# Cross-attention and FFN megakernel, one core: the third input part's norm set up ahead of the trunk, and ScalarE's copy of turned probabilities put ahead of the even step's exponential

## The reference

```
x = x + L0_xattn(keys=ctx, queries=layernorm(x), values=ctx)   # 16 heads of 64, causal softmax
x = x + L0_ffn(layernorm(x))        # FP4-quantised gate/up/down, hidden 352
x = x + L1_xattn(layernorm(x), ctx) # two softmaxes: keys 0..76 and 77..127, summed, plus bias
x = x + L1_ffn(layernorm(x))        # router, top 2 of 8 experts, hidden 512
```

## Time and profile before

| what | value |
|---|---|
| median of 3 runs | 686.27 us (685.11 to 691.33) |
| profiled execution, its own time | 689.11 us |
| its span, first to last instruction | 687.1 us |
| mean granted TensorE clock | 0.983 of full |

### The profile page before, as it was taken

One profiled execution on the slowest core, in us unless ns is written; L12 is line 12 of the kernel. 1 busy time (PEld: TensorE's weight loads), 2 busy tenths in 40 slices (PEclk: granted clock), 3 DMA queues, 4 the chain that ended last, 5 costly groups with the idle time before them and its releaser, 6 DMA issues.

```text
span 687.1 us, 16668 instructions
## 1 busy us (share of the span) xinstructions
PE 623.5 (91%) x5849; PEld 569.1 (83%) x5849; DVE 530.4 (77%) x1446; ACT 438.2 (64%) x1125; POOL 305.1 (44%) x437
## 2 busy tenths in 40 slices
PE   5788989989888999999999999999999997979980
PEld 5677878878878888999999989988888977969980
DVE  5789996788888988889899897797666675655655
ACT  4777788777777776665565655555755545646760
POOL 2465434343434343353434342335327575465550
PEclk9999999999999999999999999999999999999995
DMA  9700000000000000316666041000001001212215
GB/s 228 234 2 1 2 2 2 1 2 1 1 2 1 2 18 1 124 42 127 121 112 125 2 120 36 1 2 1 2 1 32 25 24 49 63 55 60 74 51 187
DMA packets 49470, 33.28 MB, mean 48 GB/s; under 512 B 9494, under 2 KB 45948, under 8 KB 49388
## 3 DMA queue, kind: packets, MB, share of 16 engines
q1 hardware_dynamic: 47116, 27.55, 17.1%
q0 software_dynamic: 2272, 4.67, 2.0%
HBM read 17.57 MB, written 14.63 MB: 47 GB/s over the span
## 4 chain that ended last, share of the span: by engine, by line
PE 53%; DVE 15%; issue 12%; ACT 9%; POOL 7%; DMA 2%; another core or an unknown queue 1%; SPq 0%; POOLq 0%; DVEq 0%; ACTq 0%
PE ps_s L756 6%; PE ps_j L587 6%; PE ps_h L830 5%; PE ph L1684 5%; ACT scores L968 5%; PE ps_t L794 5%; PE py L1695 4%; PE ps_j L367 4%; PE ps_h L809 4%; DVE scores L1236 4%; PE ps_j L369 3%; PE ps_j L368 3%; POOL probs L1511 3%; POOL xs_scratch L1611 3%; DVE neg_max L1243 3%
## 5 line engine op out<-in xcount | busy, mean ns | idle before, releaser
L1511 POOL TENSOR_TENSOR probs<-scores,rsums 128x308 f32<-128x308 f32 (+1 forms) x192 | 153.9, 816 | 224.9 <-DVE rsums L1256 223.8
L1251 DVE TENSOR_REDUCE sums<-scores 128x4 f32<-128x308 f32 (+1 forms) x192 | 90.7, 500 | 28.7 <-ACT scores L968 23.4
L794 PE MATMUL ps_t<-ident,probs 128*128 128x128 f32 x512 | 78.4, 275 | 24.5 <-ACT probsT L984 21.8
L968 ACT ACTIVATE scores<-scores,neg_max 128x128 f32<-128x128 f32 x256 | 81.6, 394 | 21.9 <-DVE neg_max L1243 21.7
L855 ACT ACTIVATE QT<-ps_j 128x512 f32<-128x512 f32 x64 | 38.3, 598 | 80.4 <-PE ps_j L369 80.3
L794 PEld LDWEIGHTS ps_t<-ident,probs 128*128 128x128 f32 x512 | 57.7, 140 | 31.4 <-issue 26.2
L984 ACT ACTIVATE probsT<-ps_t 128x512 f32<-128x512 f32 x128 | 75.5, 590 | 5.8 <-PE ps_t L794 5.8
L756 PE MATMUL ps_s<-KT,QT 64*128 64x128 f32 x1024 | 75.7, 288 | 0.8 <-ACT KT L861 0.8
L809 PE MATMUL ps_h<-probsT,V 128*64 128x128 f32 x1024 | 70.0, 279 | 1.2 <-DVE x_sb L1016 1.1
L756 PEld LDWEIGHTS ps_s<-KT,QT 64*128 64x128 f32 x1024 | 63.3, 190 | 8.8 <-issue 2.4
L830 PE MATMUL ps_h<-Wo,headsT 128*128 128x128 f32 x512 | 69.1, 278 | 0.0
(11 more groups left out here) (240 smaller groups left out, 1615.7 us busy)
## 6 DMA issues: line engine op xcount, KB each, us to landing
xs_scratch<-xs SPq DMA_DIRECT2D x8, 1032.0 KB, 8.3
xt<-xs_scratch SPq DMA_DIRECT2D x39, 64.5 KB
w1b<-in_L_ffn_w_dram SPq DMA_DIRECT2D x1, 2048.0 KB, 8.2
big_raw<-in_L_ffn_w_dram SPq DMA_DIRECT2D x8, 256.0 KB, 5.0
ysum<-y_scratch SPq DMA_DIRECT2D x4, 512.0 KB, 5.3
Wo<-in_L_xattn_Wo_dram SPq DMA_DIRECT2D x2, 512.0 KB, 4.9
out_dram<-x_sb SPq DMA_DIRECT2D x4, 256.0 KB, 2.3
x_sb<-in_x_dram SPq DMA_DIRECT2D x3, 256.0 KB, 9.2
```

Of the source, the lines that this page charges most:

```text
L794: ins = nc.tensor.transpose(ps_pT[:, j * S:(j + 1) * S], probs[s % 2][:, j, :], ident[:, :])
L968: ins = nc.scalar.activation(scores[s % 4][:, j, :], scores[s % 4][:, j, :], ACT.Exp, bias=neg_max[:, s % 4, 0, j:j + 1])
L1251: ins = nc.vector.tensor_reduce(sums[:, p4, i, :], scores[p4][:, :, k0:k1], AX_X, ALU.add)
L1511: ins = nc.gpsimd.tensor_tensor(probs[(s - 1) % 2][:, :, k0:k1], scores[r][:, :, k0:k1], rsums[:, r, i, :].rearrange("p (h a) -> p h a", a ...
```

## The change

Three edits.

1. The third part. VectorE's statistics(2) run ahead of the trunk, right after statistics(1), instead of in step 1. GpSimd's rstd, centring and scaling of part 2 run ahead of the trunk too, behind those of part 1 (whose scaling moves from step 0), instead of in steps 2 and 3. On SP's queue the load of x part 2 goes ahead of the three loads of weight halves 3, 4 and 5. PART_AT for part 2 is 0 instead of 1, so its transposes and ScalarE's split come in step 3 instead of 4 and VectorE's low halves in step 4 instead of 5.
2. One weight part later: w0_low(5) goes from step 1 to step 2 on VectorE.
3. In even steps of both layers ScalarE makes the copy probsT (with its waits for the transposes and for the heads) right after the copy KT and ahead of the exponential, instead of after the exponential and the slots. Odd steps are as before.

```
--- before.py
+++ after.py
@@ -381,7 +381,7 @@
         def part_of(g):
             return next(p for p, (b0, nb) in enumerate(PARTS) if b0 <= g * PAIR < b0 + nb)
 
-        PART_AT = {1: -2, 2: 1, 3: 7, 4: 11}
+        PART_AT = {1: -2, 2: 0, 3: 7, 4: 11}
         QUANT_FROM, QUANT_TO = 7, 22
         WT_AT, WT_LOW = (16, 18, 22), (17, 19)
 
@@ -485,6 +485,7 @@
             for j in (1, 2):
                 w0_low(dve, j)
             statistics(dve, 1)
+            statistics(dve, 2)
 
         def over_width(v, nb):
             return v.rearrange("p (b a) -> p b a", a=1).broadcast_to([P, nb, D])
@@ -943,6 +944,13 @@
                     router_silu(u, 2)
                     router_silu(u, 3)
 
+            def copy_probs(n, s, G, first):
+                if (s >= 2 or not first) and s - 2 < STEPS:
+                    act.wait_ge(SS["pT_ready"], n - 1)
+                    wait_pos(act, SS["heads_ready"], G * BLOCKS + (s - 6) // 2 + 1)
+                    nc.scalar.activation(probsT[(s - 2) % 4][:, :, :].rearrange("p h s -> p (h s)"),
+                                         ps_pT[:, :], ACT.Copy).then_inc(SS["pT_copied"], 1)
+
             def step(G, g, s, lay, prev, first=False, last=False, nxt=None, f=None, fd=None):
                 n = G * STEPS + s
                 if s < STEPS:
@@ -956,6 +964,8 @@
                 if s < STEPS:
                     if par == 0 and (hb + 1 < BLOCKS or not last):
                         copy_k(m + 1, (hb + 1) % BLOCKS)
+                    if par == 0:
+                        copy_probs(n, s, G, first)
                     if par == 1:
                         act.wait_ge(SS["v_ready"], m + 1)
                         wait_pos(act, SS["heads_ready"], m - 1)
@@ -978,11 +988,8 @@
                 slot(**f)
                 for u, t in routes(n):
                     route_mid(u, t)
-                if (s >= 2 or not first) and s - 2 < STEPS:
-                    act.wait_ge(SS["pT_ready"], n - 1)
-                    wait_pos(act, SS["heads_ready"], G * BLOCKS + (s - 6) // 2 + 1)
-                    nc.scalar.activation(probsT[(s - 2) % 4][:, :, :].rearrange("p h s -> p (h s)"),
-                                         ps_pT[:, :], ACT.Copy).then_inc(SS["pT_copied"], 1)
+                if s % 2 == 1 or s >= STEPS:
+                    copy_probs(n, s, G, first)
                 if s % 2 == 0 and (s >= 4 or not first) and s < STEPS + 4:
                     mr = G * BLOCKS + (s - 4) // 2
                     act.wait_ge(SS["heads_ready"], mr + 1)
@@ -1277,13 +1284,13 @@
                         if i - 2 < len(now):
                             quantise_weights(now[i - 2])
                     for p, t in parts_at(n):
-                        if t == 0 and i == 3:
+                        if t == 0 and i == 3 and n > 0:
                             statistics(dve, p)
                         if t == 4 and i == 0:
                             part_low(dve, p)
                     if n == 0 and i in (2, 3):
                         w0_low(dve, i + 1)
-                    if n == 1 and i == 2:
+                    if n == 2 and i == 2:
                         w0_low(dve, 5)
                     slot(part=i, **f)
                     slot(part=i, **fd)
@@ -1536,10 +1543,10 @@
                     nc.gpsimd.tensor_tensor(lo[:, cols], big_raw[:, cols], hi[:, cols].bitcast(F32),
                                             ALU.subtract).then_inc(split, 1)
                 for p, t in parts_at(n):
-                    if t == 1:
+                    if t == 1 and p > 2:
                         rstd_part(pool, p)
                         center_part(pool, p)
-                    if t == 2:
+                    if t == 2 and p > 2:
                         scale_part(pool, p)
                 blank(n - GROUPS * STEPS)
                 if n >= ROUTE_FROM[0]:
@@ -1618,8 +1625,10 @@
                        {124: range(0, 2), 125: range(2, 4), 126: range(4, 6), 128: range(6, 8)}]
 
             stage(0, 0, 0)
-            rstd_part(pool, 1)
-            center_part(pool, 1)
+            for p in (1, 2):
+                rstd_part(pool, p)
+                center_part(pool, p)
+                scale_part(pool, p)
             return trunk(pool, step), rstd_of, twin, send
 
 
@@ -1905,9 +1914,9 @@
             load_w0(2)
             load_x(1)
             load_ctx(1)
+            load_x(2)
             for j in (3, 4, 5):
                 load_w0(j)
-            load_x(2)
             load_ctx(2)
             sp.wait_ge(s_fz, 1)
             for i, w in enumerate((w_gate, w_up)):
```

## The result

The changed kernel took 683.92 us (median of 20 runs, 681.42 to 687.96) against 687.24 us of the kernel before in the same runs: ratio 0.9952 [0.9936, 0.9967], 3.3 us faster where 6.4 was forecast. Run again on two other occasions it gave 0.9928 [0.9902, 0.9953] and 0.9933 [0.991, 0.9956], 4.9 and 4.6 us. The direction was right; about half of the size came in the first comparison, three quarters in the others.

A forecast was written before the change was run, and what follows sets the result against it. TensorE bounds layer 1; in layer 0 TensorE, ScalarE and VectorE form one loop, VectorE fuller early. Start -3.35 and layer 0 copy -3.1, layer 1 nothing, sum to -6.4 us: 680 us, range 675.5 to 687.

The forecast's parts named there:

- The start, -3.35 (or -1.8 if the clock falls): Up to step 6: less idle time in step 3 and faster step 4 bring step 6 3.35 us earlier, or 1.8.
- The chance of 0.12 for a fall: Rival at step 4: the clock falls again, the start gives only 1.8 us, time 681.4; chance 0.12.
- The links: Steps 1 to 3: sums at about 19.4 us, copy probsT at 20.9, TensorE's new wait of about 2 us.
- The copy in layer 0, +0.6 - 3.7 = -3.1: Layer 0: probsT ahead of the exponential costs 0.6 us by step 24, then gains 3.7 in eight pairs.
- the eight named pairs: Steps 30, 32, 36, 42, 46, 52, 56, 62: the copy fits ScalarE's idle time, gaining 0.46 us each on average.
- the 0.2 us lost in 34, 44 and 54: Layer 0, these three steps: TensorE loses 0.2 us each, made good in the next pair.
- the forecast pieces: Steps 6 to 22, where VectorE is full: single losses and returns at each step, leaving +0.6 us at step 24.
- The rival by which all 21.8 us come back: Whole span: all of TensorE's wait for the copy probsT is regained, time 664.5 us; chance 0.05.
- In layer 1 I cost the edit at nothing: All of layer 1: TensorE has no gap to give and the later exponentials stay covered, so edit 3 costs 0.
- step 70: Layer 1 example: its exponential moves from 294.46 to about 296.35 us, with 0.5 us of cover before VectorE's sums.
- One sign of being wrong: After step 64: a difference to the kernel before that shrinks, instead of some 6 us unchanged to the end.

The follow-up runs named there:

- c2_changed: The changed kernel again, unedited, on the same chip as e12: 682.70 us, ratio 0.9933 to the kernel before.
- e5: The changed kernel with probsT ahead of the even exponential only up to step 4 and from 24 to 110: 680.81 us, ratio 0.9903.
- e8: The changed kernel with the copy headsT also ahead of the exponential in eight late-input pairs: 679.72 us, ratio 0.9903.
- e4: The changed kernel with part 2's transposes back in step 4 and its low halves in step 5: 684.49 us, ratio 0.9923.
- e7: The changed kernel with the edits of both e5 and e4: 680.56 us, ratio 0.9903.
- e9: The changed kernel with 14 more, unneeded matmuls in step 3 ahead of the part transposes: 682.71 us, ratio 0.9941.
- e11: e7 with the copy headsT also ahead of the exponential in six pairs of layer 0: 676.57 us, ratio 0.9857.
- e3: The changed kernel with the copy probsT back behind the exponential from step 112 on: 684.79 us, ratio 0.9915.
- e12: The changed kernel with the copy probsT back behind the exponential in steps 114 and 118 only: 680.07 us, ratio 0.9894.
- c0_changed: The changed kernel again, unedited, on another occasion: 681.98 us, ratio 0.9928 to the kernel before.
- e1_start: The changed kernel with edits 1 and 2 only, the copy probsT behind the exponential everywhere: 686.93 us, ratio 0.9955.
- c1_before: The kernel before again, unedited, for a second profile: 685.72 us, one run.
- e10: The kernel before with the copy probsT ahead of the even exponential only from step 112 on: 690.50 us, ratio 1.0052.
- e2: The changed kernel with edit 3 only, edits 1 and 2 taken back: 686.42 us, ratio 0.9949.

## Why the prediction was half right

**The start, -3.35 (or -1.8 if the clock falls): both sizes right, the credit in part misplaced.** Where step 0 took 2.08 us as in the profile of before, and the clock held in step 4, c2_changed, e5 and e8 stand at -3.65, -3.61 and -3.51 (e4, e7, e9 and e11 lie near them); where it fell, the changed kernel, e3 and e12 at -1.58, -1.81 and -1.66. What was missing is a third case, a step 0 at the full pace already: -4.97 in c0_changed. In the three profiles of the changed kernel each case came once. The chance of 0.12 for a fall was too low: of the ten profiles with the new start and a slow step 0 it fell in three; in both profiles of before it fell as well. The links (sums, copy, new wait of about 2 us) were right within 0.2 us. But the prediction had edit 3 bring the copy forward in step 3; e1_start shows that TensorE's wait shrinks without edit 3 too, since the part transposes cover the copy.

**The copy in layer 0, +0.6 - 3.7 = -3.1: right, the first term in part by luck.** The distance from step 6 to 64 changed by -3.30, -3.32 and -3.34 us in the three profiles of the changed kernel: +0.33 to step 24, -3.65 behind it. Pair by pair, from the distances of c2_changed: seven of the eight named pairs gave 0.46 to 0.71 us, pair 30 gave nothing, 0.14 us each came ahead of steps 26 and 30, and the 0.2 us lost in 34, 44 and 54 came as forecast. Ahead of step 24 the forecast pieces did not all come: step 6 was to lose 0.48 and gained 0.14, step 14 lost 0.68 for 0.5, step 16 lost 0.11 for 0.65, and 18 gave nothing back for 0.49; the errors largely cancel in the sum. e5 shows that the early part is a loss of the copy's place there (0.04 without it), e8 that headsT was the next limit, as the earlier trace rows said. The rival by which all 21.8 us come back fell with it.

**"In layer 1 I cost the edit at nothing": the step that failed.** Up to step 114 it held, at -0.2. But I followed only the loop of scores, probabilities and heads, took step 70 for all of layer 1, and looked for who waits for the exponential among VectorE's sums. Behind the exponential on ScalarE stands, in steps 114 and 118, also the router's hidT, and behind that TensorE. One sign of being wrong that the prediction named came with it: the distance shrinks after step 64, from 6.98 to 3.39 us in c2_changed. The two waits are 0.48 + 0.85 = 1.33 us. In the profiles the loss from 114 to 122 is 2.4 us (changed) and 3.8 to 3.9 us (c0, c2), where c1_before moved by 0.2; what exceeds the waits goes with the low clock. Alone it costs 3.6 us [2.0, 5.2] by e10.

**The sum.** For c2_changed: -3.65 + 0.33 - 3.67 - 0.22 + 3.83 = -3.38 us at step 122. For c0_changed -4.66, for the first profile -2.73: -3.6 in the mean, beside a measured 3.3 to 4.9. With layer 1 at nothing, as forecast, c2 would stand at -7.0, close to the -6.4. In the first profile two terms missed: the start stands at -1.58 instead of -3.35, since the clock fell there, and layer 1 at +2.1 instead of nothing (-0.21 to step 114, +2.36 behind it).

**What stays open.** How the copy's place in the routed steps brings the clock down. Of the eight profiles that have the hidT waits, seven had low clock between 490 and 550 us; of the eight without them, two. The mean granted clock of all executions, on record for every run, says the same. e10's nine lie at 0.975 to 0.978, the fourteen of before on the same chip at 0.976 to 0.982, medians 0.977 and 0.980; 0.003 of 690 us is 2.1 us, and with the waits' 1.33 that is 3.4 of the measured 3.6 (an estimate from these rows). On the chip of c0, c2, e9, e5, e7 and e12, 4 of the 35 executions with the waits reached 0.982, and 16 of the 18 without. On the chip of e1 to e4, e3 and e4 show no such distance (medians 0.980 and 0.981). So the copy's place there costs clock; that the waits are the way is not shown: e3 and e12 fell without them, e2 kept the clock with them, and in the changed kernel's first profile the fall at 522 us came 8 us behind the wait. How often each case of the start comes isn't known either, and the gain by the runs hangs on it: e1's profile, with the early clock, took 684.11 us, well under the median of its own runs (686.93), so its -5.2 us isn't what that kernel gives on the whole.

## What to carry to other kernels

When a wait is put ahead of other work on an in-order engine, list everything behind it in every kind of step, not in a typical one; the costly case may stand in two steps of a hundred. Before counting a stall as gain, read what the stalled engine needs next: 1.42 us of wait held 0.5 us of gain until headsT moved too. And compare distances step by step over two or three profiles of the same kernel: here the terms that repeated to 0.05 us were the edit's, and those that didn't held the clock.

## What the runs showed of the hardware

The clock at the start differs between executions of one kernel. Step 0's sixteen score matmuls at 11.0 us took 1.16 us in c0_changed and 2.08 us in c2_changed, whose rows are otherwise alike:

```profile
11.03 2.08 PE L757 MATMUL ps_s<-KT,QT 64*128 64x128 f32 x16 [0.78 <-ACT KT L862]
...
22.99 0.63 PE L416 MATMUL pf<-ident,ctx_sb 128*128 128x128 f32 x4 [1.88 <-DVE xnT_lo L471]
...
31.11 1.16 PE L757 MATMUL ps_s<-KT,QT 64*128 64x128 f32 x16
```

That is worth 1.3 us at step 6, and behind the same idle 1.9 us the clock fell in one of the three profiles, worth 2 us more. The level at the start is read from these lengths: the profile's clock column prints 1.00 there in every kernel, also where the same 16 matmuls took 2.08 us. The Trainium skill's page "TensorE: Matmul & The Clock Gate", Part 1, says that the point of the change varies with when the first matmul lands, by some half microsecond; the trace agrees that it varies, and differs in size: in c0_changed the matmuls are at the full pace from 11.04 us on, in c2_changed from 15.09 and in the changed kernel's first profile from 16.87.

Inside layer 1 the clock fell to 1.2 GHz behind waits of under 1 us (c2_changed, the 8 us from 512 on, behind the 0.85 us of step 118):

```profile
512.00:520.00 8.00, 8.00 (x44) 7.95 (x43) 1.46 (x4) 3.32 (x6) 5.84 (x8) 0.59 0.13 39
```

and in e12 behind next to none, as shown above. Such stretches cost 0.9 to 2.6 us each here (0.90 in e12 from step 120 to 122; 3.48 less the wait's 0.89 in c2_changed from 118 to 120), beside the 3.3 to 4.9 us of the whole edit.
